# Offsets of rows and weights in one SBUF tensor, and x3's halo columns evacuated behind both halves

## The reference

```
# layers 0 and 3
out = lax.conv_general_dilated(x, weight, window_strides=(1,), padding=[(4, 4)],
                               dimension_numbers=('NCH', 'OIH', 'NCH'), feature_group_count=4)
out = out + einsum('nd,od->no', c, c_weight)[:, :, None] + bias[None, :, None]
# layers 1 and 2
att = softmax(gelu(gelu(embedding @ W0 + b0) @ W1 + b1) @ W2 + b2)
agg_w = einsum('bk,koi->boi', att, weight[..., 0])
out = einsum('boi,bih->boh', agg_w, x) + (att @ bias_k)[:, :, None]
# the whole: x = x + layer(x), four times
```

## Time and profile before

| | |
|---|---|
| median of 3 runs | 2548.53 us (2548.13 to 2550.66) |
| the profiled execution's own time | 2548.97 us |
| its span | 2547.1 us |
| TensorE busy | 99% of the span |
| ScalarE busy | 88% |
| VectorE busy | 78% |

### The profile page before, as it was taken

How to read it: one execution, slowest core, us unless ns; L and a number is a source line. 1 busy time by engine, 2 the same in 40 slices (tenths; PEclk the granted TensorE clock), 3 DMA queues, 4 the chain that set the end, 5 groups by cost and what they waited for, 6 DMA issues and landing times.

```text
span 2547.1 us, 43755 instructions
## 1 busy us (share of the span) xinstructions
PE 2520.7 (99%) x11068; PEld 2062.1 (81%) x11068; DVE 1995.5 (78%) x5032; ACT 2252.2 (88%) x2449; POOL 16.0 (1%) x27
## 2 busy tenths in 40 slices
PE   7999999999999999999999999999999999999997
PEld 6888888888888888888888888888888888888886
DVE  8777787778777878787877778777877787888784
ACT  6889998999899989998998899899989998998895
POOL 2000000000000000000000000000000000000000
PEclk9999999999999999999999999999999999999999
DMA  7889889888888888899889888988888888888986
GB/s 257 318 332 331 328 324 334 329 328 325 332 328 327 329 333 326 325 333 328 329 326 333 330 329 324 333 329 329 325 333 329 327 327 333 325 326 333 329 312 235
DMA packets 334986, 825.56 MB, mean 324 GB/s; under 512 B 37370, under 2 KB 39426, under 8 KB 302210
## 3 DMA queue, kind: packets, MB, share of 16 engines
q1 hardware_dynamic: 332736, 823.94, 87.3%
q10 hardware_dynamic: 2242, 1.53, 0.2%
HBM read 137.97 MB, written 134.23 MB: 107 GB/s over the span
## 4 chain that ended last, share of the span: by engine, by line
PE 97%; DVE 1%; DMA 1%; ACT 1%; SPq 0%; issue 0%; ACTq 0%; DVEq 0%
PE pair L930 82%; PE quad L980 14%; PE pair L970 1%; DVE partial L754 0%; DMA x_ch<-x_ph 0%; DMA mix<-att_saved 0%; ACT x_ch L473 0%; ACT x_out L525 0%; DVE operands L790 0%; DMA x_ph<-in_small 0%; DVE operands L787 0%; DMA x_ph<-x_ch 0%; SPq L318 0%; SPq L370 0%; DVE operands L714 0%
## 5 line engine op out<-in xcount | busy, mean ns | idle before, releaser
L930 PE MATMUL pair<-operands 128*128 128x512 f32 x9216 | 2157.3, 393 | 3.4 <-DVE operands L805 1.8
L930 PEld LDWEIGHTS pair<-operands 128*128 128x128 f32 x9216 | 1722.6, 188 | 385.8 <-DVE operands L805 2.2
L473 ACT COPY x_ch<-x_in 128x1088 f32<-128x1088 f32 x255 | 556.9, 2184 | 0.0
L787 DVE CAST operands<-x_ch 128x512 fp32r<-128x512 f32 x512 | 205.4, 422 | 437.4 <-DMA x_ch<-x_ph 437.4
L525 ACT COPY x_out<-x_ch 128x1024 f32<-128x1024 f32 x252 | 524.2, 2080 | 0.2 <-DMA x_ch<-x_ph 0.2
L542 ACT ACTIVATE x_ph<-pair,bias_now 128x512 f32<-128x512 f32 x508 | 354.8, 699 | 187.6 <-PE pair L930 187.6
L533 ACT ACTIVATE x_ph<-pair,bias_now 128x512 f32<-128x512 f32 x512 | 357.5, 698 | 77.5 <-PE pair L930 69.7
L754 DVE SCALAR_TENSOR_TENSOR partial<-expert,mix,partial 128x128 f32<-128x128 f32 x1536 | 416.4, 349 | 0.0
L980 PE MATMUL quad<-operands 128*128 128x512 f32 x1536 | 372.9, 392 | 2.4 <-DVE operands L790 2.4
L805 DVE TENSOR_TENSOR operands<-x_ph,operands 128x542 fp32r<-128x542 f32 x512 | 357.7, 721 | 0.0
L980 PEld LDWEIGHTS quad<-operands 128*128 128x128 f32 x1536 | 289.7, 189 | 66.6 <-issue 3.1
(11 more groups left out here) (77 smaller groups left out, 214.2 us busy)
## 6 DMA issues: line engine op xcount, KB each, us to landing
x_ch<-x_ph SPq DMA_DIRECT2D x1024, 256.0 KB, 3.0
x_ph<-x_ch SPq DMA_DIRECT2D x512, 272.0 KB, 2.9
x_ph<-x_ch SPq DMA_DIRECT2D x512, 271.0 KB, 2.6
x_in<-in_x SPq DMA_DIRECT2D x128, 1024.0 KB, 5.7
out<-x_out SPq DMA_DIRECT2D x128, 1024.0 KB, 4.3
x_out<-in_W SPq DMA_DIRECT2D x8, 144.0 KB, 4.4
expert<-in_e ACTq DMA_DIRECT2D x2, 512.0 KB, 8.5
mix<-att_saved SPq DMA_DIRECT2D x2, 512.0 KB, 6.8
```

The costliest lines, as they stand in the source:

```text
L473: nc.scalar.copy(to, of).then_inc(x_cut, 1)
L930: mm = nc.tensor.matmul(conv_bank[g % 2], w[l][:, m, g, :], x[:, g, m * SEG:m * SEG + N], start=(m == 0 and x is hi and w is w_hi), stop=( ...
```

## The change

1. The layout of `operands`. Rows of a group get a pitch of `PITCH` = 560 words. High and low rows of a convolution stand together in `ROWS` = 4480 words, the low ones beginning 2224 words behind the high ones. The weights of a layer stand together too, low ones first, high ones 1712 words behind them; a layer's weights take `LAYER` = 3456 words. A group of weights follows at 432 words instead of 416, and 48 words (`LAST`) are left free ahead of the middle's operands. `operands` is 560 words wider.
2. The order of the three matmuls: high weights by low rows, high weights by high rows, low weights by high rows, in the convolutions and in the middle.
3. `evacuate_x3` evacuates both halves first, and then the two halo edges with one instruction each for all four phases, where it was one for each edge and half. `PARTS` is 4 instead of 6.
4. `att_t` has no tensor of its own any more, but lies in an unused part of `x3_ch`; it is used in the prologue only.

```diff
--- before.py
+++ after.py
@@ -42,6 +42,7 @@
     RUN = N // SEG
     EDGE = HALO * SEG
     ROW = N + 2 * EDGE
+    PITCH = ROW + SEG
     MARGIN = HALO * PH
     K = a["e0"].shape[0]
     DMA = 16
@@ -68,29 +69,36 @@
 
 
         NEXT_BLOCK = C + SEG
-        NEXT_GROUP = BLK * C + ROW - N
-        WEIGHTS = G * BLK * C + C
-        operands = sb("operands", [C, 4 * G * ROW + 2 * L + 4 * WEIGHTS + 2 * C], f32r)
-        ends = [0]
-
-        def operand(width):
-
-            ends.append(ends[-1] + width)
-            return operands[:, ends[-2]:ends[-1]]
-
-        x_hi, x_lo, x3_hi, x3_lo = (
-            operand(G * ROW).rearrange("c (g n) -> c g n", g=G)
-            for _ in range(4))
-        x1_hi, x1_lo = (operand(L).rearrange("c (p n) -> c p n", p=PH) for _ in range(2))
-
-
-        def in_phase(columns):
-
-            return bass.AP(tensor=columns.tensor, offset=columns.offset,
-                           ap=[columns.ap[0], [NEXT_BLOCK, BLK], [NEXT_GROUP, G], [1, C]])
-
-        w_hi, w_lo = ([in_phase(operand(WEIGHTS)) for l in range(2)] for _ in range(2))
-        m_hi, m_lo = (operand(C) for _ in range(2))
+        NEXT_GROUP = BLK * NEXT_BLOCK
+        WEIGHTS = (G * BLK - 1) * NEXT_BLOCK + C
+        TURN = 4 * SEG
+        ROWS = 2 * G * PITCH
+        LAYER = -(-2 * WEIGHTS // TURN) * TURN
+        LAST = 3 * SEG
+        operands = sb("operands", [C, 2 * ROWS + 2 * LAYER + LAST + 2 * L + 2 * C], f32r)
+
+        def operand(first, width):
+
+            return operands[:, first:first + width]
+
+        def rows_at(first):
+
+            return operand(first, G * PITCH).rearrange("c (g n) -> c g n", g=G)[:, :, 0:ROW]
+
+        def weights_at(first):
+
+            at = operand(first, WEIGHTS)
+            return bass.AP(tensor=at.tensor, offset=at.offset,
+                           ap=[at.ap[0], [NEXT_BLOCK, BLK], [NEXT_GROUP, G], [1, C]])
+
+        (x_hi, x_lo), (x3_hi, x3_lo) = ((rows_at(l * ROWS), rows_at(l * ROWS + ROWS // 2 - SEG))
+                                        for l in range(2))
+        w_lo = [weights_at(2 * ROWS + l * LAYER) for l in range(2)]
+        w_hi = [weights_at(2 * ROWS + l * LAYER + WEIGHTS) for l in range(2)]
+        MIDDLE = 2 * ROWS + 2 * LAYER + LAST
+        x1_hi, x1_lo = (operand(MIDDLE + n * L, L).rearrange("c (p n) -> c p n", p=PH)
+                        for n in range(2))
+        m_hi, m_lo = (operand(MIDDLE + 2 * L + n * C, C) for n in range(2))
 
         x_in = sb("x_in", [C, ODD, L + 2 * MARGIN])
         x_ch = sb("x_ch", [C, PH, ROW])
@@ -139,7 +147,6 @@
         total = [sb(f"total{l}", [B, 1]) for l in range(2)]
         share = [sb(f"share{l}", [B, 1]) for l in range(2)]
         att = [sb(f"att{l}", [B, K]) for l in range(2)]
-        att_t = [sb(f"att_t{l}", [K, B]) for l in range(2)]
 
         vec_part = x3_ch[:, :, :].rearrange("p q n -> p (q n)")[:, 0:B * K].rearrange(
             "p (b k) -> p b k", k=K)
@@ -157,6 +164,7 @@
         w0, w1, cw, w2, b0, b1 = ([take(width) for l in range(2)] for width in (C, C, C, K, 1, 1))
         spare = x3_ch[:, PH // 2:, :].rearrange("p q n -> p (q n)")
         h1, h2 = ([spare[:, (2 * n + l) * B:(2 * n + l + 1) * B] for l in range(2)] for n in range(2))
+        att_t = [spare[0:K, (4 + l) * B:(5 + l) * B] for l in range(2)]
         spread_g = x4_ph[:, 0, 0:G * C].rearrange("p (g c) -> p g c", g=G)
 
         pair = [ctx.enter_context(nc.psum_tensor(f"pair{n}", [C, 2, N], f32)) for n in range(2)]
@@ -249,7 +257,7 @@
         bias4_last_ready = sem("bias4_of_last_batch_ready")
         x_stored = [sem(f"x_stored{n}") for n in range(ODD)]
 
-        PARTS = 2 * 3
+        PARTS = 2 + 2
         ALL_ZEROED = 2 + 2 * 2
 
         def wait(eng, s, value):
@@ -549,12 +557,12 @@
                 for half in range(2):
                     act.wait_ge(mid_done, PH * b + PH // 2 * (half + 1))
                     phases = slice(half * PH // 2, (half + 1) * PH // 2)
-                    for to, of in ((EDGE + N, 1), (1, N - EDGE)):
-                        nc.scalar.activation(x3_ch[:, phases, to:to + EDGE - 1],
-                                             mid_bank[:, phases, of:of + EDGE - 1], ACT.Identity,
-                                             bias=bias3_now[:, :]).then_inc(x3_ready, 1)
                     nc.scalar.activation(x3_ch[:, phases, EDGE:EDGE + N], mid_bank[:, phases, :],
                                          ACT.Identity, bias=bias3_now[:, :]).then_inc(x3_ready, 1)
+                for to, of in ((EDGE + N, 1), (1, N - EDGE)):
+                    nc.scalar.activation(x3_ch[:, :, to:to + EDGE - 1],
+                                         mid_bank[:, :, of:of + EDGE - 1], ACT.Identity,
+                                         bias=bias3_now[:, :]).then_inc(x3_ready, 1)
 
             def step(b, slot, turn, first=False, last=False):
 
@@ -926,9 +934,9 @@
 
             def conv(l, g, hi, lo, done):
                 for m in range(BLK):
-                    for w, x in ((w_hi, hi), (w_hi, lo), (w_lo, hi)):
+                    for w, x in ((w_hi, lo), (w_hi, hi), (w_lo, hi)):
                         mm = nc.tensor.matmul(conv_bank[g % 2], w[l][:, m, g, :], x[:, g, m * SEG:m * SEG + N],
-                                              start=(m == 0 and x is hi and w is w_hi),
+                                              start=(m == 0 and x is lo),
                                               stop=(m == BLK - 1 and w is w_lo))
                 mm.then_inc(done, 1)
 
@@ -976,9 +984,9 @@
                 pe.wait_ge(m_split, 2 * b + 2)
                 for q in range(PH):
                     pe.wait_ge(x1_split, PH * b + q + 1)
-                    for m, x in ((m_hi, x1_hi), (m_hi, x1_lo), (m_lo, x1_hi)):
+                    for m, x in ((m_hi, x1_lo), (m_hi, x1_hi), (m_lo, x1_hi)):
                         mm = nc.tensor.matmul(mid_bank[:, q, :], m[:, :], x[:, q, :],
-                                              start=(m is m_hi and x is x1_hi), stop=(m is m_lo))
+                                              start=(x is x1_lo), stop=(m is m_lo))
                     mm.then_inc(mid_done, 1)
 
             def step(b):
```

## The result

The changed kernel takes 2559.10 us in the median of 6 runs (2558.74 to 2562.05), the kernel before 2548.61 in 6 runs beside it. The ratio is 1.0041, with a 95% interval of 1.0029 to 1.0054: **slower by 10.5 us**, twice the 5 us that the prediction took for the least that a measurement tells from no change. The profiled execution of after is one of 2559.36 us; its span is 2557.5.

The account below looks back on a forecast made before the run. It took TensorE, busy 99%, as the bound: 0.26 us a pass less 0.04 for trails leaves 0.22, over 126 passes 27.7 us; 2548.97 - 27.7 = 2521.3, said as 2521 us, range 2515 to 2546.

Parts of the forecast that it names:

- even level: TensorE's undisturbed distance between matmul starts, worked out from the middle's records: 226.7 ns, against 230.1 in the convolutions.
- difference: Offset of streamed rows against weights loaded meanwhile for the next matmul, modulo 64 words; claimed 0 gives 226.7 ns.
- break: Third matmul of blocks 0 and 1 in the kernel before, where weights being loaded lie 16 words further than streamed rows.
- 72 matmuls at 226.7 ns are 16.32 us: Convolutions of a pass on TensorE: 16.32 us instead of 16.57; with the middle, 0.26 us saved a pass.
- the trail: Uneven matmuls following a break, said to outlast it by five or six; one costs some 17 to 20 ns.
- the two trails' 0.04 us: Disturbance left in each pass by the product and the step from conv1 to conv4; 0.22 us of saving kept.
- The step itself disturbs, and not the difference: Rival: each 16-word shift of rows costs 0.015 us, three a group instead of two; 2563 us, slower; chance 0.16.
- moving both together changes nothing between them: Argument against the slower rival, if streaming and loading meet in the same memory; no size given.
- Part of it: Rival: even pace may need 512 bytes, a break staying in every block; 2527 to 2543, say 2535 us; chance 0.13.
- no effect: Rival: uneven records come from another cause, the sequencer or accumulation in the bank; 2549 us; chance 0.08.
- The halo: ScalarE's halo evacuations: 256 entries of about 0.34 us, giving ScalarE back 0.28 us a pass; directly worth nothing.
- The covers: Slack ahead of TensorE: ScalarE's for conv4's bank 0.27 us becoming 0.33; VectorE's low_x for conv1 0.49 becoming 0.36.

Follow-up runs that it names:

- e6: Kernel before with rows and weights each held at one offset, equal modulo 64 words in the convolutions (taps' shift left out): 2532.94 us.
- e5: Kernel before with rows and weights each held at one offset, 32 words apart modulo 64 (taps' shift left out): 2573.97 us.
- e13: Rows read as in the kernel before, but weights read at offsets agreeing with the rows streaming meanwhile (not the right weights): 2548.39 us.
- e9: Kernel before with closely packed weights; rows and weights loaded meanwhile agree and shift together 16 words backwards each block (computation partly left out): 2565.72 us.
- e11: Kernel before with closely packed weights; rows and weights loaded meanwhile agree and shift together 8 words forward each block (computation partly left out): 2572.2 us.
- e8: Changed kernel with low rows and high weights 64 words further, so streamed rows and loading weights agree in 512 bytes: 2559.57 us, ratio 1.0039.
- e3: Kernel before with only the change's halo evacuations (two of 60 elements behind both halves): 2549.27 us, ratio 1.0005.
- e12: Kernel before with segments of 32 columns instead of 16, wider rows, and the change's halo evacuations: 2590.15 us, ratio 1.0156.
- e4: Kernel before with the three blocks of a group taken from last to first: 2560.74 us, ratio 1.0048.
- e10: Kernel before with closely packed weights; rows and weights loaded meanwhile agree and shift together 32 words each block (computation partly left out): 2552.1 us.
- e14: e12 with the join's second copy split around an x1 evacuation and low_x written in two halves: 2546.25 us in 10 runs, ratio 0.9989.

## Why the prediction was wrong

- **The reading of the even level holds.** 226.7 ns, worked out of the middle's records, is what e6 runs at with the difference at 0, and e5, with 32 words, doesn't reach it in its steady stretch.
- **The step that failed** is "So the even level stands where the difference stays 0, and after each break come several uneven matmuls", and with it "72 matmuls at 226.7 ns are 16.32 us". A difference of 0 is needed and doesn't suffice. In the earlier trace rows every break stood next to a move, and I put the trail down to the break. e13 has the moves without these breaks and takes as long, 16.58 us for the 72 where the sum had 16.32. Taking the breaks away saved nothing, and the third move in each group, which the sum put at nothing, cost 15 ns. Nor does a trail last five or six matmuls of itself: in e13 it is three. Even e6, which never moves, took 16.38 and not 16.32, so the two trails' 0.04 us were about right (0.06).
- **The rival had the mechanism.** "The step itself disturbs, and not the difference" forecast 2563 us with a chance of 0.16. It named the third move and, with it, that `w_hi` is no longer at the offset of the high rows that it is multiplied with; which of these two sides costs is open. Its price of a move, 0.015 us, is what the steady stretch shows. Its size was off: 8 more moves in a pass at 15 ns are 0.12 us, and the chain showed 0.08, so 14 us became 10.5. The price holds in the steady groups. Over the 72, (16.65 - 16.38) / 24 = 11 ns a move in after and (16.57 - 16.38) / 16 = 12 before. The first group of a layer is unsettled whether there are moves or not (conv4's first takes 2056 ns even in e6), and moves near the start of a pass cost less on top: conv1's second group takes 2063 ns in after, 23 above even for its three moves, where the third takes 2085. Its argument against itself ("moving both together changes nothing between them") doesn't hold in e9 to e11 and e13, which move with the difference at 0 and pay.
- **Part of it** (512 bytes) falls with e8, and **no effect** with e5 and e6, in which nothing but offsets differs.
- **The halo.** Predicted about 0.34 us for each of 256 entries, measured 0.348; nothing in the sum, and e3 gives 1.0005. ScalarE was to get 0.28 us a pass back and got 40.1 / 128 = 0.31 (88% busy to 86%), which lies where TensorE doesn't wait for it.
- **The covers** were not put to the test: they were worked out for a pass 0.22 us shorter, and the pass got longer. That no wait came in at the head of conv1 or conv4 says nothing of their size. That such a cover matters, e12 shows.
- **The range** of 2515 to 2546 left out the slower case, which had 0.16. A rival that fitted the rows as well as the forecast did, as the text itself said, had only a general argument against it; that was worth less than I gave it.

Two things stay open. Why a move disturbs the matmuls that follow it was not found, nor which of its two sides does (above): the runs give its price for four moves, and no cause. And e4 pays as much for 16 moves backwards as after for 24 forwards: 0.27 / 16 = 17 ns a move over its 72, where e9, without breaks, pays 0.32 / 24 = 13 ns. In the third group it is 2077 ns, 18 a move, against 16 in e9. What its breaks have in that isn't separated.

## What to carry to other kernels

When one shape shows two prices inside one pass, list for every instruction everything that changes there, and look for the place where only one of them does; a cause read where two always change together is half a cause. Then build one kernel in which nothing changes (here e6) and one that has the one change without the other (here e13), before the layout is rebuilt. Where TensorE is the bound, as here with f32r matmuls of 512 columns that each load their weights, let the moving operand and the weights start at the same offset modulo 256 bytes, and change that offset as seldom as the algorithm allows. Before a layout that makes rows wider, count the slack of each engine behind the bound: here 0.27 us of cover, used up, turned a hoped-for gain into a loss of 1.6%.

## What the runs showed of the hardware

- The granted clock was 0.994 to 0.997 in all of these kernels, TensorE's level of 2.4 GHz; after's 0.997 is not below before's 0.996, so the loss is not one of clock.
- Matmuls of 128x512 on 128x128 weights of f32r, each with its own load, came every 226.7 ns at best in a steady row. With nothing moving and weights 32 words off the rows it is 16.73 / 72 = 232.4 ns in the mean, 5.7 more.
- In the steady groups a move of both by 16 words costs 15.0 ns forwards (before, e13, after) and 16.1 backwards (e9), by 8 words 17.5 (e11), by 32 words 10.0 (e10, e14). It is not paid in one place: in after all three distances of a block are longer (230.8, 231.7, 232.5 ns), in e14 the two behind each move (232.5 and 230.8).
- Worked out from the unrounded start times, nearly every pass of the kernels whose loop has no waits is a multiple of 6.67 ns long, to 1 ns (before mostly around 2928 of them, 19.520 us; after 2942, 19.613; e5 2958, 19.720). The passes of e12, where TensorE waits for ScalarE, are not: 38 of 124, no more than chance would give. So the engine seems to fall into step with something that turns in 6.67 ns, and a disturbance is rounded up to whole turns. If 64 words stand for one turn, 16 words are 1.67 ns, and the prices agree with that modulo a turn: one move of 16 costs 1.67 and two turns (15.0), one of 32 3.33 and one turn (10.0), two of 8 1.67 and five turns (35.0; measured 34.9), three of 16 backwards 15.0 and five turns (48.3). How many turns a move costs this doesn't say. It is a pattern in the numbers; no run isolated it.
